# Keys and values of the second cross attention, computed inside the causal attention's units instead of beside the scatters

## The reference, cut to what matters

```
x = LN(x + recurrent_attention(x))                     # layer 0, stage A
x = LN(x + retention_cross_attention(x, ctx))          # layer 0, stage A
x = LN(x + mixture_of_experts(x))                      # 8 experts, top 2: routing, scatter, stage M, gather
x = LN(x + causal_attention(x, wq, wk, wv, wo))        # layer 1, stage C
x = LN(x + cross_attention(x, ctx, mask, Wq, Wk, Wv, Wo))   # layer 1, stage E: K = ctx @ Wk, V = ctx @ Wv
x = LN(x + retrieval_ffn(x))                           # layer 1, stage D
```

## Time and profile before

| what | value |
|---|---|
| median of three runs | 1834.39 us (1830.06 to 1836.57) |
| the profiled execution | 1825.88 us, of which the span from the first to the last instruction is 1824.1 us |
| TensorE busy (matmuls) | 1535.4 us, 84% of the span |
| VectorE | 1142.7 us, 63% |
| ScalarE | 772.7 us, 42% |
| GpSimd | 560.1 us, 31% |

### The profile page before, as it was taken

One profiled execution on the slowest core, in us unless ns is written; L12 is line 12 of the kernel. 1 busy time (PEld: TensorE's weight loads), 2 busy tenths in 40 slices (PEclk: granted clock), 3 DMA queues, 4 the chain that ended last, 5 costly groups with the idle time before them and its releaser, 6 DMA issues.

```text
span 1824.1 us, 34185 instructions
## 1 busy us (share of the span) xinstructions
PE 1535.4 (84%) x12614; PEld 1360.5 (75%) x12614; DVE 1142.7 (63%) x2367; ACT 772.7 (42%) x1463; POOL 560.1 (31%) x648
## 2 busy tenths in 40 slices
PE   3678887318899999996777776999998999999997
PEld 2577775207788888895666664888887999998997
DVE  2658895400455555542688874787786777767775
ACT  4557651002444444442344443544543444444443
POOL 1346562670000000002556531111110444444444
PEclk9789998658899999998799997999999999999999
DMA  6332213735122222212122224112212454554452
GB/s 215 129 115 69 69 52 113 242 110 186 57 93 93 93 92 92 93 35 73 49 76 82 74 69 145 54 60 72 71 49 55 103 105 107 114 115 89 98 110 66
DMA packets 136045, 172.56 MB, mean 95 GB/s; under 512 B 11186, under 2 KB 116892, under 8 KB 135396
## 3 DMA queue, kind: packets, MB, share of 16 engines
q1 hardware_dynamic: 125156, 145.89, 28.2%
q0 software_dynamic: 6144, 16.41, 3.0%
q10 hardware_dynamic: 4608, 8.39, 1.3%
HBM read 115.45 MB, written 55.57 MB: 94 GB/s over the span
## 4 chain that ended last, share of the span: by engine, by line
PE 34%; DVE 7%; issue 6%; DMA 3%; ACT 1%; POOL 1%; SPq 1%; DVEq 0%; POOLq 0%; ACTq 0%
PE psum L518 12%; PE psum L1699 3%; PE psum L1683 3%; PE psum L1341 3%; PE psum L1677 2%; DMA arena_x<-wT_d 2%; PE psum L1660 2%; PE psum L485 2%; PE psum L493 2%; PE psum L477 1%; DVE arena_y L463 1%; DVE arena_y L1465 1%; PE psum L1367 1%; POOL d_g_parts L2040 1%; DVE psum L2269 1%
## 5 line engine op out<-in xcount | busy, mean ns | idle before, releaser
L2040 POOL TENSOR_TENSOR d_g_parts<-arena_w,d_g_parts 128x512 fp32r<-128x512 f32 x128 | 166.3, 1299 | 243.9 <-ACT d_g_parts L2172 230.7
L518 PE MATMUL psum<-d_v_high,d_g_parts 128*128 128x256 f32 x1024 | 202.8, 282 | 4.1 <-DVE arena_x L1832 2.8
L518 PE MATMUL psum<-d_x_parts,d_v_high 128*128 128x256 f32 x1024 | 192.6, 287 | 4.3 <-issue 2.6
L518 PE MATMUL psum<-m_w_high,m_h_parts 128*128 128x256 f32 x1024 | 188.0, 284 | 0.0
L1167 ACT ACTIVATE arena_x<-psum,b_e 128x512 f32<-128x512 f32 x128 | 88.2, 689 | 196.0 <-PE psum L518 94.9
L518 PEld LDWEIGHTS psum<-d_v_high,d_g_parts 128*128 128x128 f32 x1024 | 166.6, 189 | 5.3 <-issue 3.9
L518 PEld LDWEIGHTS psum<-d_x_parts,d_v_high 128*128 128x128 f32 x1024 | 157.7, 190 | 10.4 <-issue 4.9
L518 PE MATMUL psum<-m_xF_parts,m_w_high 128*128 128x512 f32 x512 | 159.5, 393 | 2.1 <-DVE m_xF_parts L513 2.1
L518 PEld LDWEIGHTS psum<-m_w_high,m_h_parts 128*128 128x128 f32 x1024 | 160.7, 192 | 0.0
L518 PE MATMUL psum<-m_w_low,m_h_parts 128*128 128x256 f32 x512 | 144.9, 283 | 0.0
L518 PE MATMUL psum<-d_vu_low,d_g_parts 128*128 128x256 f32 x512 | 144.6, 282 | 0.0
(11 more groups left out here) (262 smaller groups left out, 3806.7 us busy)
## 6 DMA issues: line engine op xcount, KB each, us to landing
arena_x<-wT_d SPq DMA_DIRECT2D x128, 256.0 KB
arena_y<-in_L_ffn_w SPq DMA_DIRECT2D x16, 1024.0 KB, 8.0
disp_d<-arena_w ACTq DMA_DIRECT2D x32, 256.0 KB
x_d<-arena_x SPq DMA_DIRECT2D x32, 256.0 KB, 2.3
kv_d<-arena_x SPq DMA_DIRECT2D x16, 512.0 KB
arena_x<-disp_d SPq DMA_DIRECT2D x16, 512.0 KB, 8.6
y_d<-arena_x SPq DMA_DIRECT2D x16, 512.0 KB, 8.9
arena_x<-kv_d SPq DMA_DIRECT2D x16, 512.0 KB, 3.3
```

What stands on the lines that cost most here:

```text
L518: ins = nc.tensor.matmul(dst, left[a_], right[b_], start=start and k == 0, stop=stop and k == 2, skip_group_check=True)
L2040: nc.gpsimd.tensor_tensor(K["gP"][:, s % 4, 1], K["g"][:, s % 2], K["gP"][:, s % 4, 0].bitcast(F32), ALU.subtract).then_inc(d_gl, 1)
```

## The change

The phase beside the scatters is deleted (its loads, matmuls, evictions and stores). Its operations are written into the steps of stage C, with one PSUM bank, bank 0, which before held only the transposed x3:

- TensorE does K of u0 right after the query projection of u0 and before the scores of u1, and V of u0 after the transposes of the probabilities and before the value projection. Both write bank 0, so the transpose of x3 now waits for the eviction of V of the unit before.
- ScalarE evicts K of u0 before it scales the probabilities of u2, and V of u0 before it copies the values of u0.
- SyncE issues the load of the transposed context of a unit beside that of x2, and the store of K and V two steps later.
- Stage M no longer waits for kv; stage E does, for the evictions on TensorE, for the stores on ScalarE and in e_load.

```diff
-        KV = {"cF": arena_x.take([P, 4, NC_, T]), "kv": arena_x.take([P, 2, 2, NC_ * T])}
...
-        def kv_tensor(pe):
...
-                project_features(bank(4 + u.p), "L1_xattn_Wk", KV["cF"][:, u.c % 4])
-                project_rows(bank(6 + u.p), "L1_xattn_Wv", KV["cF"][:, u.c % 4]).then_inc(kv_p, 1)
...
-        add("scalar", kv_scalar)
-        add("tensor", kv_tensor)
...
         def m_tensor(pe):
             pe.wait_ge(r_slots, 1)
-            pe.wait_ge(kv_s, 2 * UNITS)
-            for k in range(2):
-                pe.wait_ge(kv_st[k], 16 * per_parity)
...
+        arena_x.reset(13312)
+        KV = {"cF": arena_x.take([P, 2, NC_, T]), "kv": arena_x.take([P, 2, 2, NC_ * T])}
...
         def c_sync(sp):
                     sp.dma_start(C["x2"][:, u.p], x2_u[u.n]).then_inc(c_in[u.p], 16)
+                    done(sp, kv_p, u.back(2), 2)
+                    sp.dma_start(KV["cF"][:, u.p].rearrange("p c t -> p (c t)"), cF_d[u.n]).then_inc(kv_in[u.p], 16)
+                u = t.at(2, UNITS)
+                if u:
+                    done(sp, kv_s, u, 2)
+                    sp.dma_start(kv_d[u.n], KV["kv"][:, u.p]).then_inc(kv_st[u.p], 16)
...
                     done(pe, c_x3, u0)
-                    done(pe, c_x3F, u0.back(1))
+                    done(pe, kv_s, u0.back(1), 2)
                     to_feature(bank(0), C["x3"][:, u0.c % 4]).then_inc(c_x3T, 1)
                     done(pe, c_x3F, u0)
                     project(u0, 1, "L1_attn_wq", c_q, (c_qt, c_q2))
+                    landed(pe, kv_in, u0)
+                    project_features(bank(0), "L1_xattn_Wk", KV["cF"][:, u0.p]).then_inc(kv_p, 1)
...
                 if u0:
+                    seq_done(pe, kv_s, u0, 0)
+                    project_rows(bank(0), "L1_xattn_Wv", KV["cF"][:, u0.p]).then_inc(kv_p, 1)
                     done(pe, c_vs, u0.back(1))
...
+                if u0:
+                    seq_done(act, kv_p, u0, 0)
+                    landed(act, kv_st, u0.back(2))
+                    nc.scalar.activation(KV["kv"][:, u0.p, 0], bank(0), ACT.Copy).then_inc(kv_s, 1)
                 if u2:
                     done(act, c_sum, u2)
...
+                if u0:
+                    seq_done(act, kv_p, u0, 1)
+                    nc.scalar.activation(KV["kv"][:, u0.p, 1], bank(0), ACT.Copy).then_inc(kv_s, 1)
```

More of the change, by code:

```diff
@@ L971, in r_tensor @@
             nc.tensor.matmul(bank(1), table("ones"), oh, start=True, stop=True).then_inc(r_rank, 1)
-        KV = {"cF": arena_x.take([P, 4, NC_, T]), "kv": arena_x.take([P, 2, 2, NC_ * T])}
-        kv_in = [sem(f"kv_in_{k}") for k in range(4)]
-        kv_p, kv_s, kv_st = sem("kv_p"), sem("kv_s"), sem2("kv_st")
-        def kv_tensor(pe):
[L981 to L988, removed]
-                project_features(bank(4 + u.p), "L1_xattn_Wk", KV["cF"][:, u.c % 4])
-                project_rows(bank(6 + u.p), "L1_xattn_Wv", KV["cF"][:, u.c % 4]).then_inc(kv_p, 1)
[L991 to L999, removed]
         def r_sync(sp):
@@ L1017, in r_sync @@
             m_weights(sp, Unit(0, 2))
[L1019 to L1028, removed]
         def r_gpsimd(pool):
@@ L1113, in m_tensor @@
             pe.wait_ge(r_slots, 1)
-            pe.wait_ge(kv_s, 2 * UNITS)
-            for k in range(2):
-                pe.wait_ge(kv_st[k], 16 * per_parity)
+            for s, per in ((a_dec, 1), (a_thx, 1), (a_xF, 1), (a_cF, 1), (a_vs, 1), (a_qr, 1), (a_qp, 2), (a_kt, 2),
+                           (a_r2, 1), (a_sc, 1), (a_lg, 1)):
+                pe.wait_ge(s, UNITS * per)
+            pe.wait_ge(s_late, 16 * N_LATE)
             def step(t):
@@ L1280, in decoder @@
         C_LAG = 4
+        arena_x.reset(13312)
+        KV = {"cF": arena_x.take([P, 2, NC_, T]), "kv": arena_x.take([P, 2, 2, NC_ * T])}
+        kv_in, kv_p, kv_s, kv_st = sem2("kv_in"), sem("kv_p"), sem("kv_s"), sem2("kv_st")
         def c_sync(sp):
@@ L1580, in e_load @@
             landed(sp, c_st, u)
+            landed(sp, kv_st, u)
             sp.dma_start(X["x4"][:, u.p], x4_u[u.n]).then_inc(x_in[u.p], 16)
@@ L1646, in e_tensor @@
                 pe.wait_ge(part, UNITS)
+            pe.wait_ge(kv_s, 2 * UNITS)
             pe.wait_ge(x_one, 6)
@@ L1766, in e_scalar @@
         def e_scalar(act):
+            for k in range(2):
+                act.wait_ge(kv_st[k], 16 * per_parity)
             def exps(u, b, half):
```

## The result

The changed kernel takes 1879.09 us (median of four runs, 1877.52 to 1881.23); the kernel before takes 1832.22 us (four runs, 1826.89 to 1836.57; the three of the median above and one more). The ratio is 1.027, interval 1.024 to 1.030: slower by 46.9 us. The profiled execution of the changed kernel took 1881.23 us, its span is 1879.5 us.

The account below looks back on a forecast made before the run. Stage C was taken to be bound by a chain of waits, with GpSimd alone busy during the scatters. Stage C's 86 us less 46 us saved gave +40 us, 1875 us on the 1834.4 us median; range 1856 to 1905 us.

Parts of the forecast that it names:

- The start of the experts: Behind the scatters: with the phase gone, TensorE starts the experts at 414 to 421 us, saving 46 us.
- upper bound: Latest start of the experts: SyncE held until 416.07 us as ScalarE was, TensorE starts at 420.9, 42.9 us saved.
- lower bound: Earliest start of the experts: load 1 us after the last scatter, first transposes at 414.2, 49.6 us saved.
- K in front of the scores: Stage C step: ScalarE's in-order eviction of K delays scaling and keys' copy, so the scores start 4.48 us late.
- V in front of the values: Stage C step: V's matmuls ahead of the value projection cost 1.74 us on TensorE; their eviction costs nothing.
- A step at full clock: Stage C step: 13.28 + 4.48 + 1.74 = 19.50 us, TensorE's own queue setting the pace.
- The clock: Stage C: today's falls cost 0.26 us a step; rival: every step loses 1.2 to 2.4 us more, chance 0.12.
- Stage C in all: Whole stage: 65.5 + 14.6 + 6.2 = 86 us longer, bounds 80 and 95 us.
- Transfers: SyncE's added load and store per stage C step, and new waits at stage E's head, cost nothing.
- ScalarE's order costs nothing: Rival for stage C: the two groups only lengthen TensorE's queue; 16.74 us a step, about 1832 us; chance 0.06.
- Faster: Rival for stage C: K and V fall into TensorE's holes, 5 us in all, 1793 us; chance 0.05.
- The saving does not come: Rival at the experts' start: something unseen behind kv holds it; at half the 46 us, 1898 us; chance 0.04.

Follow-up runs that it names:

- e1: The changed kernel with only ScalarE's eviction of K moved behind the copy of the keys; 1821.8 us, 0.995 against the kernel before.
- e6: The changed kernel with only K's matmuls moved behind the transposes and its eviction behind the keys' copy, V left in place; 1797.3 us, 0.984 against the kernel before.
- e4: The changed kernel with K's matmuls behind the transposes, V's behind the attention product, evictions behind the copies TensorE awaits; 1786.9 us, 0.975 against the kernel before.
- e2: The changed kernel with the causal mask's matmul issued ten times, ahead of the waits before the scores; 1858.0 us, 1.014 against the kernel before.
- e3: The changed kernel without the matmuls and evictions of K and V, their loads and stores kept; 1788.0 us, 0.975 against the kernel before.

## Why the prediction was right, and where its sizes were off

The forecast was 1875 us with slower at 0.91; measured were 1879 us, slower by 2.7%. The forecast stood on a median of 1834.4 us for the kernel before; against the 1832.2 us of the four runs the difference is 46.9 us, where I had said 40. Step by step:

- **The start of the experts** came at 413.03 us, just ahead of my range of 414 to 421. My upper bound took ScalarE's hold-up until 416.07 us for one that might meet SyncE too. It did not: the load went out at 409.10 us, 1.4 us after the last scatter ended. The middle between the bounds was the wrong choice, the lower bound nearly the right one, and the term of 46 us should have been 50.8. Against the lower bound (414.2 us) the last scatter ended 0.6 us sooner, SyncE took 0.4 us more than the 1 us that I had allowed, and TensorE followed the load by 3.93 us in place of 4.87. Some 3.7 us of the 50.8 were gone when stage C began, since the experts' stage took 407.0 us in place of 403.2. In the six experiments it took 404 to 408 us. The cause is open.
- **K in front of the scores** was priced at 4.48 us a step, of which 2.87 us a hole of TensorE. The hole is 2.67 us, and it comes by the way described: K's group, K's eviction, scaling, keys' copy, mask. It is 0.2 us shorter than summed because the eviction starts 0.04 us after K's group, not 0.12, and the scaling 0.49 us behind the eviction, not 0.62. e1, in which only the eviction moves, has no hole there. The page "TensorE: Matmul & The Clock Gate" of the Trainium skill, section "Architectural detail: the array is 16× 32×32, not 1× 128×128", calls ScalarE's queue strictly first in, first out; the traces agree, as L1401 and L1406 stand behind the waiting L1397 in all twelve steps, and L1406 waits for nobody once e1 puts it ahead.
- **V in front of the values** was priced at 1.74 us on TensorE's queue. In the changed kernel the next group follows V's by 1.74 us (906.27 to 908.01). e6 puts its place at 1.0 us a step once the scores are in time, and TensorE's waits for the layer norm, up to 0.70 us in e4, are gone there.
- **A step at full clock** was 19.50 us by the sum and 19.22 us in the step at 913.87. TensorE no longer waits ahead of the transposes, as foreseen.
- **The clock** is the term that was mis-sized. I carried today's 0.26 us a step over unchanged, 3.1 us in twelve steps; the steps averaged 20.51 us, 1.29 us over the full-clock step, 15.5 us in twelve. Of these 12.4 us more, the shorter step at full clock gave 3.4 back, and the twelve steps came out 9 us over the sum. The rival had asked for another 1.2 to 2.4 us in every step. It came in ten of twelve steps, at some 1.5 us each, so it came true in part, and my chance for it was only 0.12. e2 shows the cause: with work in the hole the falls are gone. I had argued that 2.87 us is shorter than the 4.36 us of the earlier trace rows; the rows above show a hole of 2.67 us followed by a fall in one step and by none in the next, so the length of a hole alone does not tell.
- **Stage C in all** got 93.9 us longer, where the sum said 86 with bounds of 80 and 95. The first three steps gave 13.2 us (14.6 predicted), the twelve 74.5 us (65.5 predicted), the end 6.2 us (6.2 predicted). The end's agreement has the cause that I gave. Its window has a clock of 0.95 in both kernels, and 6.0 of the 6.2 us lie between the last transpose and the second mask behind it, where the late scores and V stand: 16.33 us before (1078.02 to 1094.35), 22.33 us here (1118.73 to 1141.06). The first row is from the kernel before:

```profile
1094.35 0.38 PE L1361 MATMUL psum<-causal_bf,ident_bf 128*128 128x512 bf16 x1 [2.96 <-POOL arena_y L1304]
```

```profile
1141.06 0.38 PE L1336 MATMUL psum<-causal_bf,ident_bf 128*128 128x512 bf16 x1 [2.96 <-POOL arena_y L1277]
```

- **Transfers** cost what I said, nothing that the steps show, as e3 tells. Its end, longer by 5.3 us, is the clock's: the output projection's group takes 2.00 us before the clock falls and 3.78 us after it.

The errors partly cancel: the saving was 1 us better at the head of stage C than the forecast's 46 (47.0), the stage 8 us worse. 93.9 - 47.0 = 46.9 us, where I had 40. That the medians are also 46.9 us apart, to the tenth, is luck, since they come from several executions and the stages from one of each kernel. The term for the start was 4.8 us too small, and the experts' stage, which I had left unchanged, took 3.7 of it back. The direction and the two large terms rest on waits that the rows show.

**The rivals.** "ScalarE's order costs nothing" described e1, not the change: 16.74 us a step and about 1832 us there, against 16.4 and 1821.8 measured. "Faster" described e4: it forecast 1793 us if K and V fell into TensorE's holes, and in e4 they do, at 1787 us. "The saving does not come" is refuted by the load at 409.10 us.

**What stays open.** In the kernel before ScalarE's evictions waited 36.7 and 29.0 us beside the scatters. I did not try what held them. L997 waits there for the unit's matmuls and for the landing of the store of two units back, and the profile calls the releaser only "remote". Open are also the 3.7 us of the experts' stage, the late transfers of stage D, and why the clock fell in ten of twelve like steps and not in the other two.

## What to carry to other kernels

Work that moves into another loop must be placed twice: its matmuls where TensorE waits for somebody, and its eviction behind every copy that TensorE waits for. Here 3.46 us of work made a step 6.2 us longer in the wrong place, and not longer at all in the right one. Look at an in-order engine's instruction ahead of the critical copy: what it waits for is then on the critical path, whatever it does itself. And where a change gives TensorE a new wait in every step, count the slower clock behind it as a term of its own, not as a rival: here a third wait of 2.67 us beside those of 1.40 and 1.24 us brought a fall in ten of twelve steps, while the two alone (e1) brought none.

## What the runs showed that I had not expected

- A loop with more matmuls ran faster than one without them: e4 takes 13.91 us a step with 3.46 us of work more than the kernel before (14.30) or e3 (14.41), at a clock of 1.00 against 0.97 and 0.96.
- Ten useless matmuls in a hole took 21 us off the median (1879.1 to 1858.0).
- GpSimd issues its scatters at one pace in both kernels, mostly 1.28 us apart (60 of the 63 distances lie between 1.27 and 1.33 us in each), with and without matmuls, evictions and on average 40 GB/s more of transfers beside them (164 against 124).
- Stage D, with the same instructions in each kernel, took from 399.0 to 413.7 us, the longer the more VectorE waited for one transfer (11.2 to 50.1 us). A difference of 10 us between two profiled executions of this kernel has to be traced to its stage before it is explained.
